# Twenty-two filler transposes of TensorE before the first transposes of a graph kernel

## The reference

```
edge_index = jnp.stack([src, dst])
x = _layernorm(x + _L0_gnn_ref(x, edge_index, weight, bias))      # one GCN step, symmetric 0/1 adjacency
x = _layernorm(x + _L1_gnn_ref(x, edge_index, W1, b1, W2, b2, W3, b3))  # three GCN steps, edges counted
x = _layernorm(x + _L2_gnn_ref(x, edge_index, Wq, bq, ...))       # masked attention
x = _layernorm(x + _L3_gnn_ref(x, edge_index, W1, b1, W2, b2))    # two GCN steps, relu between
```

## Time and profile before

| | |
|---|---|
| median of 3 runs | 538.28 us (538.21 to 538.35) |
| the profiled execution: its own time | 538.34 us |
| its span, from first to last instruction | 536.5 us |
| TensorE busy | 525.2 us (98%) |
| VectorE busy | 403.8 us (75%) |
| ScalarE busy | 171.6 us (32%) |
| GpSimd busy | 142.9 us (27%) |

### The profile page before, as it was taken

One profiled execution on the slowest core, in us unless ns is written; L12 is line 12 of the kernel. 1 busy time (PEld: TensorE's weight loads), 2 busy tenths in 40 slices (PEclk: granted clock), 3 DMA queues, 4 the chain that ended last, 5 costly groups with the idle time before them and its releaser, 6 DMA issues.

```text
span 536.5 us, 6800 instructions
## 1 busy us (share of the span) xinstructions
PE 525.2 (98%) x2276; PEld 369.9 (69%) x2276; DVE 403.8 (75%) x885; ACT 171.6 (32%) x360; POOL 142.9 (27%) x135
## 2 busy tenths in 40 slices
PE   8999999999999999999999999999999999999995
PEld 6655555457888888888774864567688888888643
DVE  7899999889788989355577977997887715790165
ACT  6999898570021022220120000542353000121100
POOL 3000000094319404032234900663400480000021
PEclk9999999999999999999999999999999999999999
DMA  8824000000202012000000000000010500000012
GB/s 287 282 80 156 2 2 0 2 0 1 42 11 107 1 20 79 0 1 1 1 0 0 1 0 2 0 0 1 8 73 0 138 0 1 0 2 0 1 59 101
DMA packets 13511, 19.63 MB, mean 37 GB/s; under 512 B 4257, under 2 KB 4513, under 8 KB 13474
## 3 DMA queue, kind: packets, MB, share of 16 engines
q1 hardware_dynamic: 13474, 19.16, 11.4%
HBM read 17.05 MB, written 2.11 MB: 36 GB/s over the span
## 4 chain that ended last, share of the span: by engine, by line
PE 73%; DVE 14%; ACT 6%; issue 4%; POOL 1%; DVEq 1%; POOLq 0%; ACTq 0%
PE bank L937 14%; PE bank L764 13%; PE bank L941 12%; PE bank L782 11%; PE bank L993 8%; PE bank L838 4%; ACT apart L1099 3%; DVE count L1369 3%; PE bank L643 3%; PE bank L655 2%; DVE hot_key L1353 1%; DVE wk_rows L1564 1%; DVE xs L1502 1%; PE bank L965 1%; DVE stats L1493 1%
## 5 line engine op out<-in xcount | busy, mean ns | idle before, releaser
L545 POOL TENSOR_TENSOR rstd<-veps,mhalf 128x1 f32<-128x1 f32 x32 | 22.3, 696 | 175.4 <-DVE veps L1495 172.6
L782 PE MATMUL bank<-adj,y_hi 128*128 128x512 f32 x128 | 50.8, 397 | 0.0
L782 PE MATMUL bank<-adj,y_lo 128*128 128x512 f32 x128 | 50.7, 396 | 0.0
L1502 DVE SCALAR_TENSOR_TENSOR xs<-bank,dinv,xs 128x512 f32<-128x512 f32 x23 | 16.9, 748 | 43.9 <-PE bank L838 30.5
L1369 DVE TENSOR_TENSOR count<-bank,count 128x160 f32 x128 | 41.4, 323 | 5.7 <-issue 2.9
L1099 ACT ACTIVATE apart<-col_lo,edge_key 128x128 bf16<-128x128 int16 x128 | 44.0, 396 | 0.7 <-PE bank L675 0.7
L582 POOL TENSOR_SCALAR mask<-count 128x1024 bf16<-128x1024 uint16 x8 | 23.5, 2932 | 49.8 <-DVE peak L1714 42.1
L1353 DVE TENSOR_TENSOR hot_key<-col_key,key 128x320 bf16<-128x320 int16 x128 | 35.3, 317 | 0.3
L687 PEld LDWEIGHTS bank<-hot_key,lo_near 128*128 128x128 bf16 x128 | 12.2, 98 | 33.4 <-issue 25.2
L647 PE MATMUL bank<-w_sb,x0t 128*128 128x512 f32 x64 | 33.1, 604 | 0.8 <-ACT wqt L1093 0.6
L1106 ACT ACTIVATE lo_far<-apart,ones 128x256 bf16<-128x256 bf16 x64 | 32.0, 501 | 0.0
(11 more groups left out here) (290 smaller groups left out, 1239.2 us busy)
## 6 DMA issues: line engine op xcount, KB each, us to landing
w_sb<-in_L_gnn_W_dram SPq DMA_DIRECT2D x3, 1024.0 KB, 5.6
xs<-in_x_dram SPq DMA_DIRECT2D x2, 1024.0 KB, 7.0
v_sb<-in_L_gnn_W_dram SPq DMA_DIRECT2D x2, 1024.0 KB, 6.6
out_dram<-xs SPq DMA_DIRECT2D x7, 256.0 KB, 2.0
w_sb<-in_L_gnn_weight_dram SPq DMA_DIRECT2D x4, 256.0 KB, 6.0
wq_sb<-in_L_gnn_Wq_dram SPq DMA_DIRECT2D x1, 1024.0 KB, 10.4
wk_sb<-in_L_gnn_Wk_dram SPq DMA_DIRECT2D x1, 1024.0 KB, 12.9
wq_rows<-in_L_gnn_Wq_dram SPq DMA_DIRECT2D x1, 1024.0 KB, 7.8
```

Of the source, the lines that this page charges most:

```text
L782: mm = pe.matmul(to, y[part][:, k, f * P:(f + 1) * P], m[:, k, half], start=n == 0 and part == 0 and m is mat, stop=n == NB - 1 and part = ...
```

## The change

Both calls of the helper and the helper itself go; every other instruction of every engine stays as it is and in its order.

```
-            def idle_turns(count_):
-
-                for n in range(count_):
-                    pe.transpose(bank[:, HALF + 3, 0:P], ident[:], ident[:])
-
             pe.wait_ge(const_set, 1)
-            idle_turns(16)
             for n in range(3):
                 if n < 2:
                     pe.wait_ge(act_rows_set, n + 1)
                 else:
-                    idle_turns(6)
                     pe.wait_ge(rows_set, 1)
                 for c in range(CPG):
                     at_col = ((n % 2) * CPG + c) * G
```

## The result

The kernel without its fillers takes 541.07 us (median of 5 runs, 540.11 to 541.62), the kernel before 538.21 us (538.07 to 538.35). The ratio is 1.0041 with a 95% interval of 1.0021 to 1.0060. It is slower by more than a measurement needs to tell, by 2.2 us as a ratio and 2.9 us by the medians, and it scatters five times as widely. The forecast was 539.0 us, "within 0.2%", with a range up to 540.4. It was wrong. The direction was right, and the rival "the rise comes late" is what happened.

A forecast was written before the change was run, and what follows sets the result against it. The prediction took the opening's chain of waits, with TensorE at half clock until about 6.8 us, as the bound. A 0.7 us later "xw" made 538.34 + 0.7 = 539.04, said as 539.0 us; range 538.1 to 540.4.

The forecast's parts named there:

- the rise comes late: Rival: TensorE's clock rises behind about 11.3 us, slowing the matmul and "xw"; 540.0 to 540.6 us, chance 0.26.
- The bounds of the chain: Opening: set 2 at 6.83 and x at 7.65 us allow at most 0.5 us of the 4.5 us of filler.
- The clock at half pace before the rise, and no level on record: TensorE until about 6.8 us: 1.2 GHz, transposes every 0.227 us against 0.117; the column's 1.00 means no level recorded.
- Part (d): Opening on TensorE: without fillers the clock rises at 10.2 us, slowing real work; "xw" starts at about 11.6, not 10.89.
- the sum of +0.7 us: Whole kernel: "xw" starts 0.7 us later and the end moves by as much, 538.34 + 0.7 = 539.04 us.
- Three times within 0.14 us: Runs of the kernel before: so small a spread speaks for a clock rise at a fixed point, though three are few.
- at most doubled: "xw" on TensorE: a 512-column matmul at the slow level takes at most twice its time.
- the bound of 0.63: Matmul with `group_dia` on TensorE: the slow level adds between 0 and 0.63 us; 0.28 was forecast.
- the slack: VectorE's path from `group_row` to group 3's one-hots: 0.85 us before TensorE takes them, so its 1.0 us delay stays hidden.
- What hides it: Chain from "xw" at 10.89 us to the end: no hole seen, so the 0.7 us shift passes through whole.
- taken up: Rival: slack in the ring of four slots or ScalarE's queue leaves 0 to 0.3 us at the end; 538.4 us, chance 0.12.
- outer bound: Extreme of the late rise: the clock never rises before "xw" ends, at 17.8 in place of 13.6 us, +4.2 us.

The follow-up runs named there:

- 16 + 12: Kernel before with twelve fillers in place of six in front of set 2: 538.49 to 539.42 us in ten runs, 540.90 in one.
- 16 + 6: The kernel before, unedited, with sixteen and then six fillers: 537.85 to 539.00 us in 86 runs, 540.02 to 542.06 in 7.
- the wide ones: Kernel before with two 512-column matmuls for the sixteen fillers, and four transposes or none for the six: ratios 1.0014 and 1.0007.
- 16 + 2 + 2: Kernel before with its six fillers split, two before set 2 and two before x's transposes: six runs 538.02 to 538.30 us, six 540.15 to 541.41.
- 16: Kernel before without the six fillers, the sixteen kept: 537.81 to 538.25 us in 7 runs, 540.46 to 541.01 in 14.
- half rows: Kernel before with 28 and 10 fillers over 64 rows and 64 columns in place of 16 and 6: 540.36 to 541.65 us in 7 runs.

## Why the prediction was wrong

**The bounds of the chain: right.** That the 4.5 us of filler on the chain of waits could not be won held. Set 2's transposes ran at 6.97 and x's at 7.70, both as worked out (6.9 and 7.7). The four of set 2 ended near 7.65 and not at 7.4, so that `distances` and `keyed` came 0.32 us sooner (7.78 against 8.10, 7.75 against 8.07) and not 0.55; neither bounds anything here.

**The clock at half pace before the rise, and no level on record: right.** Transposes of x came at (1.97 - 0.42) / 7 = 0.22 us.

**The place of the rise: the step that failed.** Part (d) took the 4.8 us from the kernel before, counted them from 5.4 us and had the rise at 10.2. It is at 13.6 in the profiled run, and in none of the 14 profiles between 8.0 and 13.6. So "xw" started at 12.54 and not at 11.6, its own pieces were partly slow, and the sum of +0.7 us became +1.77 in the profiled run and +2.9 by the medians. The assumption under it, that the rise follows the first work by a length that one trace shows, has no support: sixteen full fillers from 2.0 us on are followed by an early rise in some runs and not in others. The transposes of x from 7.7 us on did not bring it within the time of the forecast in any profile.

**Three times within 0.14 us as a sign that the rise stands still: misjudged.** 7 of 93 runs of the kernel before are late, and three of three early ones is the likely draw. The Trainium skill, "TensorE: Matmul & The Clock Gate", section "Part 1: The HAM clock gate", says that the point of release may differ from run to run of one kernel. I held the three times against that; the runs agree with it. Early rises at 5.7 to 6.8 us cost nearly the same, 537.95 to 538.34 us in six profiles. Why, I can only argue: the fillers and the wait for x lie where the clock comes up, and take up the difference.

**The sizes: right where the rise is given.** The late rival had +2.2 us on "xw" for a rise at 13.6. Measured were +2.16 at unit 4's copy, and +1.8 at the end. A 512-column matmul at the slow level was not in the trace of before; the bound "at most doubled" holds but for a few hundredths: the longest record is 2.02 times the median (all of line L647 in the kernel after):

```profile
L647 PE MATMUL bank<-w_sb,x0t x64: 592/593/1196, 12.5 to 78.7; 128*128 128x512 f32 x64
```

The matmul with `group_dia` took 10.75 - 9.60 = 1.15 us against 0.63, 0.52 more where I had 0.28, since it lay at the slow level throughout; both lie under the bound of 0.63. `group_row` came 1.2 us late, inside the slack.

**What hides it: right in the main.** The prediction had nothing hidden; 0.36 us are, between unit 4 and the end. The rival "taken up" is out as more than that.

**The chances.** The late rise had 0.26 and the range stopped at 540.4, in the middle of that rival's own times (540.0 to 540.6) and far under its outer bound (+4.2 us, 542.5). The runs of the kernel after lie between 540.11 and 541.77, all inside that bound. With one trace for where the rise falls, and a cost that grows with each microsecond it comes later, the range should have held the whole of the rival.

**What stays open.** What exactly TensorE must have done for the rise, and why full fillers from 2.0 us sometimes don't suffice. The runs only order the versions: early were 10 of 11 with 16 + 12 and 86 of 93 with 16 + 6, then 9 and 8 of 12 with the wide ones, 6 of 12 with 16 + 2 + 2, 7 of 21 with 16, and none with half rows. No profile of a late run of a version with full fillers from 2.0 us was had, and six such runs have a lower mean clock than the others, which speaks for a second way to be late. Whether wide fillers raise the clock more surely than transposes isn't settled by 12 runs.

## What to carry to other kernels

Filler on the chain of waits is not won time: look at the pace of equal instructions ahead of and behind it, because a column of the granted clock may have no entry for the opening. Here only filler over the whole array went with an early rise; small or half-height instructions did nothing, though there were more of them. And where a cost depends on something that differs from run to run, time the version many times and list the single runs: a median of 538.2 and one of 541 can be one program.

## What the runs showed of the hardware

- The same program with the same inputs fell in two groups, 537.81 to 538.25 and 540.46 to 541.01 us, with nothing between, on one core alone (21 runs on two chips).
- The clock first rose by 8.0 us in seven profiles (5.7 to 8.0) and at 13.6 us or later in seven (13.6 to 16.6), never between.
- Sixteen 128x128 transposes in 3.68 us from 2.0 us on were followed by a rise to the 2.4 GHz level before 8 us in 7 of 21 runs by the times (at 5.7 and 6.3 us in the two that were profiled); with six more behind them in 86 of 93. Twenty-eight transposes over 64 rows in 3.25 us and ten more were followed by none in 7 runs.
- At the 1.2 GHz level a transpose of 128 columns came every 0.22 us against 0.117, a MATMUL record of 512 float32 columns lasted up to 1222 ns against 593, and its weight load up to 338 ns against 190.
- TensorE was busy for 5.90 of the 5.90 us from 7.7 to 13.6 in the changed kernel, and at half clock all that time.
